# Cross-attention and quantised feed-forward on one core: a reordered batch step, a spread handoff, and 1024-column exponentials and products

## What is computed

```
q = layernorm(x); k = v = ctx                      # 16 heads of 32
ig, fg = [q,k,v] @ Wi + bi, [q,k,v] @ Wf + bf
log_D[s,t] = cumsum(log_sigmoid(fg))[s] - cumsum(...)[t] + ig[t],  t <= s
D = exp(log_D - rowmax)
C = (q k^T / sqrt(32)) * D                         # per head, 256 x 256, causal
h = C v / max(|sum C|, exp(-rowmax));  hn = layernorm over the 32 features of a head
x1 = x + hn * ln_scale
y  = layernorm(x1)
out = x1 + q_act(silu(q_act(y) @ q_w(Wg)^T) * (q_act(y) @ q_w(Wu)^T)) @ q_w(Wd)^T
```

## Time and profile before

| | |
|---|---|
| median of 3 runs | 550.96 us |
| time of the profiled execution | 553.07 us |
| its span, first to last instruction | 551.3 us |
| mean granted PE clock | 0.837 |
| PE busy | 454.0 us (82%) |
| DVE busy | 432.6 us (78%) |
| ACT busy | 244.9 us (44%) |
| POOL busy | 245.2 us (44%) |

### The profile page before, as it was taken

The page is one execution under the profiler, slowest core; times in us unless marked ns, Lnnn a source line. Parts: engine busy times, 40 slices in busy tenths (PEclk is TensorE's granted clock), DMA queues, the critical chain, the costliest instruction groups (busy, mean ns, idle before and its releaser), DMA issues.

```text
span 551.3 us, 10415 instructions
## 1 busy us (share of the span) xinstructions
PE 454.0 (82%) x3465; PEld 300.7 (55%) x3465; DVE 432.6 (78%) x615; ACT 244.9 (44%) x343; POOL 245.2 (44%) x231
## 2 busy tenths in 40 slices
PE   0597795599789696969788785399999999999984
PEld 0497795287657484757566562144444444444441
DVE  3769888478797897978787965997788788788880
ACT  2466664247264353545364544234434344344341
POOL 2444531323635536273736563543454443443433
PEclk9767886589859586776859697899999999999996
DMA  6655621412321414050421101201111111112111
...
DMA packets 30564, 43.70 MB, mean 79 GB/s; under 512 B 6980, under 2 KB 11972, under 8 KB 30532
## 3 DMA queue, kind: packets, MB, share of 16 engines
...
## 4 chain that ended last, share of the span: by engine, by line
PE 42%; issue 20%; POOL 17%; DVE 13%; ACT 4%; DMA 3%; POOLq 1%; SPq 1%; DVEq 0%; ACTq 0%
PE psA L1335 9%; PE psC L1362 9%; PE psA L1344 9%; PE psB L1354 3%; POOL wq L559 3%; POOL early L616 3%; PE psA L1234 2%; PE psC L1214 2%; DMA early<-in_x_dram 2%; POOL xc L649 2%; DVE wy L952 2%; DVE wq L955 1%; POOL qs L644 1%; PE psC L1173 1%; POOL rs L553 1%
## 5 line engine op out<-in xcount | busy, mean ns | idle before, releaser
L679 POOL TENSOR_TENSOR kTa<-kTa,ps 128x1024 bf16<-128x1024 bf16 x32 | 61.2, 1912 | 102.7 <-DVE kTa L1116 102.7
L1262 PE MATMUL psA<-vp,DC 128*128 128x128 f32 x512 | 73.7, 312 | 2.1 <-DVE DC L1019 2.1
L559 POOL TENSOR_TENSOR wq<-wq,ws 128x1024 bf16<-128x1024 bf16 x24 | 50.6, 2108 | 54.9 <-DVE wq L955 54.9
L1262 PEld LDWEIGHTS psA<-vp,DC 128*128 128x128 f32 x512 | 71.4, 227 | 4.0 <-issue 4.0
L1335 PE MATMUL psA<-WgT,qTa 128*128 128x512 bf16 x256 | 63.7, 394 | 7.5 <-ACT hf L813 3.9
L1362 PE MATMUL psC<-WdT,kTa 128*128 128x512 bf16 x256 | 62.2, 387 | 2.4 <-ACT kTa L879 2.4
L1344 PE MATMUL psA<-WuT,qTa 128*128 128x512 bf16 x256 | 61.3, 383 | 0.0
L879 ACT ACTIVATE kTa<-psB 128x1024 bf16<-128x1024 bf16 x32 | 32.8, 1024 | 54.5 <-PE psB L1354 54.2
L1019 DVE SCALAR_TENSOR_TENSOR DC<-psA,DC 128x512 f32<-128x512 f32 x64 | 41.7, 686 | 15.7 <-PE psA L1234 8.3
L1104 DVE TENSOR_TENSOR kTa<-kTa,psA 128x1024 f32<-128x1024 f32 x32 | 39.0, 1220 | 18.2 <-PE psA L1344 18.2
L804 ACT ACTIVATE DC<-psB 128x512 f32<-128x512 f32 x64 | 37.6, 597 | 23.6 <-PE psB L1248 23.2
...
## 6 DMA issues: line engine op xcount, KB each, us to landing
...
```

The costliest lines, as they stand in the source:

```text
L559: nc.gpsimd.tensor_tensor(blocks(wq[p][:, :]), blocks(wq[p][:, :]), spread(ws4[p][:, :], UB), ALU.mult).then_inc(wq_ready.sem, 1)
L679: nc.gpsimd.tensor_tensor(blocks(pd[h]), blocks(pc[h]), spread(ps4[h][:, :], PB), ALU.mult).then_inc(pq_ready.sem, 1)
L1262: last = nc.tensor.matmul(psA[:, j, to:to + P], DC[n % DCN][:, i4 * P:(i4 + 1) * P], values[:, left:left + P], start=i4 == 0, stop=c == 0, ...
```

## The change

**Pairs.** The ring of six buffers and the two banks of `psB` each become one tensor, and `exps` and `c_mult` treat two groups n = 2m, 2m+1 in one instruction of 1024 columns: four of each per batch in place of eight. `decay` of either group of a pair waits until the exponential of the pair before has been taken; `heads` waits for the product of its pair.

**Order within a batch.** On POOL the multiplication by `ln_scale` leaves `residual` and becomes `scale_h`, which works in place on the heads before normalisation and stands first in the step; `w_back` of the first unit moves ahead of `residual`, and `weigh` ahead of the second `w_back`. On ACT `x1_norm` moves from before `copy_h(b, 1)` to behind all exponentials of batch b+1's first chunk; the evacuations of weights move back too. On PE both `w_transpose` move to later places. On DVE the second `w_front` moves ahead of `x1_stats`.

**Handoff.** The last batches' `head_norm`, `x1_stats`, `x1_round`, `x1_norm`, `x_transpose` and `evac_xq` are spread over tiles 0 to 5. The inverse root of batch 7's variances is one `pow` on POOL (`last_power`) instead of ACT's guess and a correction.

**Prelude.** The constants are loaded from ACT's queue, `w_front(0)` stands ahead of `x_stats(1)`, the tables are built after the second `x_rsqrt`, one `w_transpose` moves behind the last gates, `qk(0, 0)` goes ahead of the wait for the decays, and the decays' DMAs signal one semaphore per chunk and parity instead of one for all.

```
-        DC = [sb(f"DC{n}", [P, HC * P]) for n in range(DCN)]
+        ring = sb("ring", [P, DCN, HC * P])
+        DC = [ring[:, n, :] for n in range(DCN)]
-        psB = [st.enter_context(nc.psum_tensor(f"psB{i}", [P, 512], F32)) for i in range(2)]
+        expo = st.enter_context(nc.psum_tensor("psB", [P, 2, 512], F32))
+        psB = [expo[:, i, :] for i in range(2)]
...
@@ POOL, attention step @@
+            def last_power(b):
+                gp.wait_ge(hv_ready.sem, hv_ready.at(b, 1))
+                nc.gpsimd.tensor_tensor(sm[:, 0].rearrange("p c h -> p (c h)"), sm[:, 3].rearrange("p c h -> p (c h)"),
+                                        mhalf[:, 0:1].broadcast_to([P, NCH * NH]), ALU.pow).then_inc(hr_ready.sem, 1)
+            def scale_h(b, p):
+                gp.wait_ge(sq_ready.sem, sq_ready.at(b, 1))
+                settle(gp)
+                own = hf[p][:, :, :, 0:DH]
+                nc.gpsimd.tensor_tensor(own, own, lns[:, :].rearrange("p (h d) -> p h d", d=DH).unsqueeze(1)
+                                        .broadcast_to([P, NCH, NH, DH]), ALU.mult).then_inc(hs_ready.sem, 1)
             def residual(b):
                 gp.wait_ge(hn_ready.sem, hn_ready.at(b, 1))
-                ch.link(nc.gpsimd.tensor_tensor(hn, hn, lns[:, :].unsqueeze(1).broadcast_to([P, NCH, E]), ALU.mult))
...
             def step(b, p, n, first, last):
                 if not first:
+                    scale_h(b - 1, 1 - p)
                     head_rsqrt(b - 1)
+                w_back(2 * b + B + 1, 1)
                 if not first:
                     residual(b - 1)
                 if not last:
                     carry_q(b + 1, 1 - p)
-                w_back(2 * b + B + 1, 1)
                 if not first:
                     x1_rsqrt(b - 1)
                 if not last:
+                    weigh(b + 1, 1 - p)
                     w_back(2 * b + B + 2, 0)
-                    weigh(b + 1, 1 - p)
                 if not first:
                     back_x(b - 1)
@@ POOL, handoff @@
+            scale_h(B - 1, 1)
+            last_power(B - 1)
+            back_p(0, 0)
+            back_p(0, 1)
             residual(B - 1)
+            back_p(1, 0)
+            back_p(1, 1)
+            add_x1(0, 0, 0)
             x1_rsqrt(B - 1)
...
@@ ACT @@
+            def exps(b, m):
+                k = 2 * m % DCN
+                act.wait_ge(d_mm.sem, d_mm.at(b, 2 * m + 2))
+                nc.scalar.activation(ring[:, k:k + 2, :], expo[:, :, :], ACT.Exp).then_inc(d_exp.sem, 1)
             def step(b, p, n, first, last):
-                evac_gate_up(2 * b + B, 0, b)
                 if not first:
                     head_power(b - 1)
                 copy_h(b, p, 0)
-                exps(b, 4)
-                exps(b, 5)
+                exps(b, 2)
+                evac_gate_up(2 * b + B, 0, b)
                 copy_v(b, p, 1)
+                copy_state(b, p)
+                exps(b, 3)
                 if not first and not (isinstance(b, int) and b == 1):
                     evac_xq(b - 2)
-                copy_state(b, p)
-                exps(b, 6)
-                exps(b, 7)
                 if not last:
                     round_const(2 * b + B + 2, 0)
-                if not first:
-                    x1_norm(b - 1)
                 copy_h(b, p, 1)
-                evac_gate_up(2 * b + B + 1, 1, b)
                 if not last:
                     exps(b + 1, 0)
+                    copy_v(b + 1, 1 - p, 0)
                     exps(b + 1, 1)
-                    copy_v(b + 1, 1 - p, 0)
-                    exps(b + 1, 2)
-                    exps(b + 1, 3)
+                if not first:
+                    x1_norm(b - 1)
+                evac_gate_up(2 * b + B + 1, 1, b)
                 square(b, p)
@@ DVE @@
+            def c_mult(b, m):
+                k, j = 2 * m % DCN, 2 * m % HPC
+                ve.wait_ge(qk_done.sem, qk_done.at(b, 2 * m + 2))
+                ve.wait_ge(d_exp.sem, d_exp.at(b, m + 1))
+                nc.vector.scalar_tensor_tensor(out=ring[:, k:k + 2, :], in0=psA[:, j:j + 2, :], scalar=float(DH) ** -0.5,
+                                               in1=ring[:, k:k + 2, :], op0=ALU.mult, op1=ALU.mult).then_inc(c_ready.sem, 1)
...
                 if not last:
                     w_pow(2 * b + B + 2, 0)
+                    w_front(2 * b + B + 3, 1, b + B // 2 + 1)
                 if not first:
                     x1_stats(b - 1)
                 if not last:
-                    w_front(2 * b + B + 3, 1, b + B // 2 + 1)
                     w_round(2 * b + B + 2, 0)
                 if not first:
                     x1_round(b - 1)
@@ DVE, handoff @@
             pair(0, 0)
-            x1_stats(B - 1)
             pair(0, 1)
-            x1_round(B - 1)
+            head_norm(B - 1, 1)
             pair(1, 0)
             pair(1, 1)
+            x1_stats(B - 1)
+            pair(2, 0)
+            pair(2, 1)
+            pair(3, 0)
+            x1_round(B - 1)
+            pair(3, 1)
@@ PE @@
             def decay(b, p, n):
                 c, j = divmod(n, HPC)
-                if n == 0:
-                    pe.wait_ge(d_ld, 16 * NCH * (1 + SPLIT) * b + 16 * NCH * (1 + SPLIT))
+                if j == 0:
+                    pe.wait_ge(d_ld[p][c], 16 * (1 + SPLIT) * (b // 2 + 1))
                 if not (isinstance(b, int) and b == 0 and n < 2):
-                    pe.wait_ge(d_exp.sem, d_exp.at(b, n - 1))
+                    pe.wait_ge(d_exp.sem, d_exp.at(b, n // 2))
...
             def step(b, p, n, first, last):
-                w_transpose(2 * b + B, 0, rows_order)
                 for k in range(HPC):
                     heads(b, p, k)
                 decay(b, p, 4)
                 decay(b, p, 5)
+                w_transpose(2 * b + B, 0, rows_order)
                 centre(b, 1)
                 qk(b, 1)
+                state(b)
+                decay(b, p, 6)
+                decay(b, p, 7)
                 if b >= 2:
                     pe.wait_ge(wT_ev.sem, wT_ev.unit(2 * b + B))
                     x_transpose(b - 2)
-                state(b)
-                decay(b, p, 6)
-                decay(b, p, 7)
                 for k in range(HPC, 2 * HPC):
                     heads(b, p, k)
                 inter(b, p)
-                if b >= 2:
-                    pe.wait_ge(xqT_ev.sem, xqT_ev.at(b - 2, 1))
-                w_transpose(2 * b + B + 1, 1, rows_order)
                 if not last:
                     decay_qk(b + 1, 1 - p)
                     centre(b + 1, 0)
                     decay(b + 1, 1 - p, 2)
                     decay(b + 1, 1 - p, 3)
+                if b >= 2:
+                    pe.wait_ge(xqT_ev.sem, xqT_ev.at(b - 2, 1))
+                w_transpose(2 * b + B + 1, 1, rows_order)
```

More of the change, by code:

```diff
@@ L592, in pre_step @@
                     x_rsqrt(b + 1)
+                if first:
+                    tables()
+                    gate_weights()
                 if not first:
@@ L890, in tile @@
                     silu(t, h)
+                    if h == 0 and moved is not None:
+                        evac_xq(moved)
+                if normed is not None:
+                    x1_norm(normed)
                 y_copy(t - 1, p)
@@ L1070, in step @@
             def step(b, p, n, first, last):
-                for k in range(HPC):
-                    c_mult(b, k)
+                for m in range(2):
+                    c_mult(b, m)
                 if not first:
@@ L1194, in pre_step @@
                     gates(b - 1)
-                    w_transpose(b - 1, 1 - p, cols_order)
+                    if not last:
+                        w_transpose(b - 1, 1 - p, cols_order)
             for b in range(B):
@@ L1199, in _ @@
             gates(B - 1).then_inc(gate_mm, 1)
-            w_transpose(B - 1, 1, cols_order)
+            for b in (B - 2, B - 1):
+                w_transpose(b, b % 2, cols_order)
             pe.wait_ge(gn_ready, 1)
@@ L1370, in tile @@
                     up(t, b, q, h)
+                    if h == 0 and moved is not None:
+                        if t > 2:
+                            pe.wait_ge(y_ev.sem, y_ev.at(t - 2, 1))
+                        x_transpose(moved)
                     down(t - 1, 1 - q, h)
@@ L1377, in _ @@
                 up(0, 0, 0, h)
[L1378 to L1382 removed]
+            tile(1, 0, 1, moved=B - 2)
+            pe.wait_ge(xqT_ev.sem, xqT_ev.at(B - 2, 1))
+            for t in range(2, 6):
+                tile(t, t // 2, t % 2, moved=B - 1 if t == 5 else None)
             pe.wait_ge(xqT_ev.sem, xqT_ev.at(B - 1, 1))
[L1384 removed]
+            with pe.Fori(0, TILES // 2 - 3) as i:
                 for p in range(2):
[L1386 removed]
+                    tile(2 * i + 6 + p, i + 3, p)
             for h in range(2):
```

123 lines of the change are left out of this document (55 added, 68 removed).

## The result

The changed kernel takes 563.08 us in the median of five runs (559.50 to 565.43), the kernel before 550.96. The ratio is 1.019, with a 95% interval of 1.0115 to 1.0265: slower by about 2%, where the interval leaves open on which side of 2% it lies. A second series of six runs gave 560.43 against 550.12, ratio 1.020 (1.0152 to 1.0247). The forecast was 558.5 in a range of 543 to 573, with 0.52 on no change and 0.38 on slower. In what follows the ratios are of fast runs, while the medians of e3 and e4 include one slow run each (553.57 and 593.13), without which they are 548.16 and 567.22.

What follows compares the result with a forecast made beforehand. A loop of waits between engines, none of them full, was taken to set the batch. Period +6.3, batch 1 +5.4, prelude 0 and handoff -4.1 sum to +7.6 us on 553.07: 560.7, as a median 558.5, range 543 to 573.

Steps and rivals of the forecast that it cites:

- Period: Middle batches, first product to first product: 32.0 us against 30.74, +1.26 each, five times, +6.3 us.
- 1.6 of collision: head_var's first small DVE instruction waits beside POOL's back_x and scale_h: 1.6 us, bounds 0 and 2.4.
- 0.5 a batch for a low clock: PE's second heads at 1.2 GHz after idle time: 0.5 us a batch taken, bounds 0 and 1.77.
- rival 2: Clock falls ahead of every second heads: 1.77 a batch for 0.5, 565 us, up to 580; chance 0.22.
- The loop's partner: POOL's residual, carry_q, x1_rsqrt chain ends about 24.7 us into the batch, hidden; its collisions use DVE's slack.
- Batch 1: Batch 1, scale_h wholly ahead of head_var and PE at low clock: 35.2 against 29.8, +5.4 us, bounds +1.5 and +6.
- Prelude and batch 0: Stages up to batch 1's first product: 0 us taken, bounds -3 and +1.5.
- Joining: Products of 1024 columns for two of 512: saves 0.06 us per pair, 0.24 per batch; 0.16 per pair by the skill.
- Handoff: Last batch into feed-forward: first gate 1.1 sooner, 3.2 back at x1_round; -4.1 us, bounds -4.6 and +4.3.
- last_power: POOL's pow of 32 elements at the handoff: between 0.70 and 11.2 us, 2.8 taken, 0.5 us lost.
- rival 3: pow costs by the element: 11.2 us on POOL with DVE's L930 held behind it, 567 us; chance 0.13.

Runs made afterwards that it cites:

- e3: The kernel before with only the changed kernel's spread handoff, batch order and 512 columns kept: 548.31 us, ratio 0.995.
- e4: The changed kernel with scale_h behind head_rsqrt on POOL in place of ahead of it: 568.43 us, ratio 1.0299.
- e1: The changed kernel with exponentials and products made for one head group again (512 columns), all orders kept: 555.64 us, ratio to before 1.0106.
- e5: The changed kernel with only x1_stats moved ahead of the second w_front on DVE: 560.03 us, ratio 1.0198.
- e7: The changed kernel with x1_stats ahead of the second w_front and x1_norm between the pair's two exponentials: 556.01 us, ratio 1.0107.
- e8: e7 with w_front's reductions ahead of head_var and x1_stats, first w_pow behind x1_stats, and copy_v and round_const moved on ACT: 554.19 us, ratio 1.0122.
- e9: e8 with exponentials and products of 512 columns again: 556.49 us, ratio 1.0126.
- e10: e3 with scale_h in every batch, w_front's reductions and x1_stats placed earlier on DVE: 540.42 us, ratio 0.9841.
- e12: e10 with copy_h and the next batch's first exponential ahead of x1_norm on ACT, evacuation behind the second exponential: 534.01 us, ratio 0.9689.
- e2: The kernel before with only its exponentials and products joined to 1024 columns, all orders kept: 555.27 us, ratio 1.0116.
- e11: e8 with head_norm behind the third and fourth products in place of ahead of them: 558.36 us, ratio 1.0177.
- again: The changed kernel itself traced a second time, nothing changed: span 557.4 us, period 31.56.

## Why the prediction was right, and where its terms were off

The forecast was +7.6 us on the profiled execution and came out at +6.4; the mechanism of its period, `x1_norm` behind the second exponential and DVE waiting for it, is the one that the trace and e1, e5 and e7 show. That the sum is so near is in part luck: the period was put 2.3 us too high and the handoff's gain 1.2 too high, and the two errors work against each other. As a median the forecast of 558.5 is 4.6 below the measured 563.08.

- **Period, +6.3 forecast, +4.0 measured.** L1052 took 1.78 us where 2.3 was forecast (the 0.71 of before and 1.6 of collision). So the third product ended 13.96 us after the first one's start (14.5 forecast) and `inter` at 18.94 (19.5); with 0.28 us of waiting for POOL `x1_norm` ended at 26.9 (27.1), and the way from there to the next batch took 4.6 (4.41). This gives the 31.5 that the prediction had at full clock. The mis-sized term is the 0.5 a batch for a low clock: the second `heads` took 3.81 at full clock in each of batches 2 to 6, after gaps of 0.06 to 1.36 us, so it is 0 in the changed kernel, and rival 2 did not come there. Its mechanism is real all the same: it came in batches of e4, e5, e8 and e9, at 1.2 to 1.8 us each.
- **The loop's partner.** The prediction had POOL's chain end at 24.7 and hidden. It ended at 25.35, since L547 and L548 took 0.94 and 1.20 beside DVE's `w_round` for 0.2 each. That is why moving `x1_norm` alone should not have helped (no run did that alone); the prediction called the collisions with `w_pow` and `w_front` DVE's slack and missed that DVE's work also stands on POOL's chain.
- **Batch 1, +5.4 forecast, +5.7 measured.** This is the largest term, and its inner steps are in the trace. All of `scale_h` lies ahead of L1056, which is L1029 in before, and the second `heads` run low:

```profile
133.89 2.17 POOL L619 TENSOR_TENSOR hf<-hf,lns 128x1024 f32<-128x1024 f32 x1 [0.71 <-ACT early L843]
133.96 2.17 DVE L1056 TENSOR_TENSOR sm<-sm,gT 128x32 f32<-128x32 f32 x1 [0.71 <-ACT early L843]
...
146.21 5.62 PE L1296 MATMUL psA<-vp,ring 128*128 128x128 f32 x32 [3.10 <-DVE ring L1046]
```

From the first product at 129.42, `scale_h` ended at 6.6 (6.8 forecast), `head_var` at 8.5 (8.9), `head_norm` at 15.5 (15.5), `inter` at 23.4 (23.2), `x1_norm` at 31.0 (30.8). The low clock cost 1.8 (1.5 forecast). No run changed one of these steps by itself; e10, with the old orders of ACT and PE, has 28.5 there.
- **Prelude and batch 0, 0 forecast, -0.3 measured.** The spread of the first product over traces with the same prelude, 106.3 to 113.1, is wider than the bounds that the prediction set (-3 and +1.5), so this term is neither confirmed nor refuted.
- **Joining, 0.24 a batch gained.** Two products of 1024 take 2.35, four of 512 take 2.47 in e12: 0.12 per half batch, as forecast, and not the 0.32 that the prediction gives beside it as 0.16 per pair. It is no gain in the period: at like clocks joining costs nothing in e1's order and 0.2 to 0.5 us a batch in those of e2 and e9, and in the medians it costs (e1, e2). The prediction had no term for that.
- **Handoff, -4.1 forecast, -2.9 measured.** The first gate came 0.5 us sooner (1.1 forecast). The gates gained 6.4 and `x1_round` took 4.0 back (3.2 forecast). PE's rows show it as 1.20 + 2.83:

```profile
401.40 1.90 PE L1380 MATMUL psA<-WuT,qTa 128*128 128x512 bf16 x8 [1.20 <-DVE kTa L1131]
...
407.86 0.61 PE L1390 MATMUL psB<-identb,kTa 128*128 128x128 bf16 x8 [2.83 <-POOL kTa L688]
```

- **last_power.** 5.41 us, between the bounds of 0.70 and 11.2 and twice the 2.8 taken; rival 3 (11.2, DVE held behind it) was wrong on both counts: DVE's small instructions ran inside it, as the last section shows.
- **Of the medians**, 10 to 12 us lie between the kernels where the traces show 6.4. Before's profiled execution lies 0.4% above its median; both of the changed kernel's are the lowest of their series. Which stage has the difference in the other runs isn't known. The cost of joining that e1 and e2 show by their medians may be part of it, and so may second `heads` at a low clock in some of their batches; neither was tested.

## What to carry to other kernels

When an engine waits, look whether a second chain ends just behind the one that the trace names: e1 and e5 each shortened one of two and gained nothing and 0.5 us a batch, e7 had to shorten both. Where DVE and POOL both work from SBUF, a POOL step is not free because POOL is idle; it is free beside DVE's reductions and its products from PSUM. e10 has `scale_h` so placed and gains; how much of that is the placing isn't shown, since no run has `scale_h` in the old order without it. A shorter wait at a handoff is worth what is left after the moved work is paid at its new place: 7.8 us gained and 3.9 paid in e3. And before a mean period is compared, look at PE's clock batch by batch: in e4, e5, e8 and e9 it moves a batch by more than most of the edits do.

## What the runs showed of the chip

- DVE and POOL block each other both ways, and for whole instructions: 0.18 became 1.83 (e7, ended with POOL's `w_back`), 1.21 became 3.20 (e4), POOL's 0.24 became 1.08 to 1.12 (e8). DVE's reductions (1.19 to 1.22), `bn_stats` (0.67 to 0.70 each) and products from PSUM (1.19 to 1.23 for 1024 columns) kept their times beside POOL in every trace. The Trainium skill (SBUF — State Buffer, section "SBUF: two separate sides") calls the shared port pair an exclusive lock, taken by a DVE instruction in a 2-port mode or with two SBUF inputs, the latter only against a GpSimd instruction that reads SBUF, as all of these do. The rows agree; for L957 and `w_pow`, which have one input, no row shows the mode.
- One row does not: during POOL's `pow` on 128x32 elements DVE's small instruction and a product of two SBUF tensors ran at their usual 0.18 and 1.23. The other way round `pow` did wait: the one on 128x2 elements, 0.71 in the changed kernel, took 1.78 beside such a product in e8 and e11. Whether the 5.41 holds a wait of this kind is open, as DVE's work beside it is the same in every trace with it.

```profile
351.81 5.41 POOL L612 TENSOR_TENSOR sm<-sm,mhalf 128x32 f32<-128x32 f32 x1
...
354.15 0.18 DVE L953 TENSOR_SCALAR ps<-pam 128x32 int32<-128x32 int32 x1
...
354.70 1.23 DVE L1140 TENSOR_TENSOR qTa<-kTa,pinv 128x1024 fp8e4<-128x1024 f32 x1 [0.15 <-DVE pinv L956]
```

- PE's clock falls and comes back within a batch, and where it falls can differ for the same instructions (before and e3, above). In e4 the `heads` after 1.20 us without work took 3.81 at a granted clock of 1.00, those after 1.88 us 5.44; but in batch 1 of e12 2.11 us still gave 3.81, and in e5 1.43 us gave 5.44, so the length of the gap alone does not tell.
- The time up to batch 0's first product was between 106.3 and 113.1 us in the six traces of kernels that share the changed prelude and the 1024 columns (changed, again, e4, e5, e7, e8), against 31.55 and 31.56 for the period of the two that are the same kernel.
